# An attention and mixture-of-experts block: the routing stage written out per group of tokens, with a new order of work

## The reference, cut to what matters

```python
x = x + attn(layernorm(x))      # q, k, v = x @ wq.T, ...; 16 heads of 8
# qf, kf = elu(q) + 1, elu(k) + 1;  kv = sum over s of kf * v
# out = (qf @ kv) / (qf . sum(kf) + 1e-6);  then @ wo.T + bo
x = x + ffn(layernorm(x))       # 16 experts, top 2 of z @ router_w.T
# gates = sigmoid(top 2 logits)
# expert: (silu(z @ gate) * (z @ up)) @ down, scaled by the gate
# plus one shared expert of width 256 over all tokens
```

## Time and profile before

| what | value |
|---|---|
| median of 3 runs | 284.52 us (281.02 to 284.95) |
| profiled execution, span | 282.7 us (the page gives no other time for it) |
| PE busy, DVE busy, ACT busy, POOL busy | 214.7, 167.2, 124.3, 162.1 us |
| first scatter of the dispatch starts | 48.0 us |
| last scatter of the dispatch starts | 136.4 us |
| first block of the expert stage, PE | 145.3 us |
| last scatter of the expert stage starts | 255.7 us |

### The profile page before, as it was taken

One profiled execution on the slowest core, in us unless ns is written; L12 is line 12 of the kernel. 1 busy time (PEld: TensorE's weight loads), 2 busy tenths in 40 slices (PEclk: granted clock), 3 DMA queues, 4 the chain that ended last, 5 costly groups with the idle time before them and its releaser, 6 DMA issues.

```text
span 282.7 us, 5194 instructions
## 1 busy us (share of the span) xinstructions
PE 214.7 (76%) x1218; PEld 174.8 (62%) x1219; DVE 167.2 (59%) x670; ACT 124.3 (44%) x324; POOL 162.1 (57%) x164
## 2 busy tenths in 40 slices
PE   1677878887677557359949979899799799795561
PEld 0346676876566455247846768588587587594561
DVE  3337969678697787544326647647457466321582
ACT  2726465667648533050204635536455455420010
POOL 0454001757757666777301777777777777772780
PEclk9988959599999998856989999999999999999595
DMA  4225810111111111117733233333333333103993
GB/s 151 74 74 134 372 74 1 57 40 47 47 41 57 47 48 39 49 57 149 96 78 86 80 88 96 107 98 88 97 97 94 92 103 98 53 6 92 327 343 130
DMA packets 27876, 27.61 MB, mean 98 GB/s; under 512 B 4782, under 2 KB 25525, under 8 KB 27730
## 3 DMA queue, kind: packets, MB, share of 16 engines
q1 hardware_dynamic: 21954, 17.99, 22.4%
q0 software_dynamic: 4608, 8.47, 9.5%
q10 hardware_dynamic: 1296, 0.94, 1.6%
HBM read 15.70 MB, written 12.73 MB: 101 GB/s over the span
## 4 chain that ended last, share of the span: by engine, by line
PE 44%; DVE 17%; issue 12%; POOL 12%; DMA 8%; ACT 4%; SPq 1%; POOLq 0%; DVEq 0%; ACTq 0%
POOL routed L347 9%; PE pKVN L994 9%; PE pZ L988 6%; PE pQ L988 6%; DMA routed<-Z,ROWS 4%; PE pT L980 4%; PE pKV L853 3%; PE pT L983 3%; PE pZ L951 2%; POOL results L360 2%; PE pKVN L922 2%; DVE Z L558 2%; PE pKVN L843 2%; PE pN L843 2%; DVE c_stat L516 2%
## 5 line engine op out<-in xcount | busy, mean ns | idle before, releaser
L360 POOL DMA_INDIRECT results<-Y,XS x80 | 78.7, 984 | 40.5 <-ACT Y L466 21.3
L347 POOL DMA_INDIRECT routed<-Z,ROWS x64 | 62.0, 969 | 47.2 <-DVE ROWS L650 29.5
L730 DVE COPY xhT<-pT 128x256 f32<-128x256 f32 (+1 forms) x83 | 34.4, 414 | 20.6 <-PE pT L983 16.0
L994 PE MATMUL pKVN<-WF,xhT 128*128 x160 | 35.3, 302 | 1.5 <-ACT Y L466 1.5
L994 PEld LDWEIGHTS pKVN<-WF,xhT 128*128 128x128 f32 x160 | 26.3, 188 | 16.1 <-issue 14.5
L466 ACT ACTIVATE Y<-pKVN,XS 128x128 f32<-128x128 f32 x80 | 29.4, 367 | 5.6 <-PE pKVN L994 2.1
L980 PE MATMUL pT<-CN,XS 128*128 128x128 f32 x80 | 23.1, 289 | 11.4 <-issue 6.7
L853 PE MATMUL pKV<-WF,sh_h 128*128 128x128 f32 x128 | 20.9, 307 | 8.2 <-DVE X L746 8.2
L853 PEld LDWEIGHTS pKV<-WF,sh_h 128*128 128x128 f32 x128 | 19.1, 217 | 9.6 <-DVE sh_h L741 8.8
L988 PE MATMUL pZ<-WF,xhT 128*128 x80 | 24.8, 392 | 0.0
L988 PE MATMUL pQ<-WF,xhT 128*128 x80 | 24.4, 387 | 0.0
(11 more groups left out here) (124 smaller groups left out, 429.7 us busy)
## 6 DMA issues: line engine op xcount, KB each, us to landing
XS<-routed SPq DMA_DIRECT2D x80, 65.0 KB, 1.9
YL<-results SPq DMA_DIRECT2D x16, 256.0 KB, 5.8
WF<-w_ffn SPq DMA_DIRECT2D x1, 3456.0 KB, 12.0
X<-x SPq DMA_DIRECT2D x8, 256.0 KB, 2.7
out<-X SPq DMA_DIRECT2D x8, 256.0 KB, 2.9
results<-Y,XS POOLq DMA_INDIRECT x80, 2.3
routed<-Z,ROWS POOLq DMA_INDIRECT x64, 2.3
routed<-pad SPq DMA_DIRECT2D x11, 65.0 KB, 4.3
```

The source lines that it names most:

```text
L347: nc.gpsimd.indirect_dma_start(routed, bass.IndirectOffsetOnAxis(ap=ROWS[:, par, t, k:k + 1], axis=0), Z[:, par, t, k, :], None).then_inc( ...
L360: nc.gpsimd.indirect_dma_start(results, bass.IndirectOffsetOnAxis(ap=XS[:, j, D:D + 1].bitcast(U32), axis=0), Y[:, j, :], None, bounds_che ...
L730: nc.vector.tensor_copy(xhT[:, j % 2, a:b, :], pXH[:, a:b, :]).then_inc(s_xhT, 1)
L994: nc.tensor.matmul(pY, xhT[:, (j + 3) % 2, 1, :], WF[:, 2 * EXP_DIM:][:, bass.ds(w, D)], start=True, stop=True).then_inc(s_D, 1)
```

## The change

The two places of Z become eight, one for each quad, and so do the row numbers `ROWS`; the tile ZB that holds them is the same memory as `YL` of the end, which takes the place of a tile of its own. `norm2` no longer waits for scatters. The token numbers, which `route` copied into Z quad by quad (L610), are copied in one instruction before step 0. All eight loads of X are issued one behind the other, with a semaphore for each quad, and `WF` right behind them. PSUM's Z is copied straight into `ZT`, from which the logits are now computed; `zT` and its second copy are gone. The loop over pairs of steps, which made one turn, and POOL's loops are written out.

The order within a step changes on three engines. PE: state, keys, queries, numerators, transpose of Z, transpose of the tokens, logits, transpose of the attention, output projection, and the ranks of s-2 at the end of the step (before: of s-3, in the next step, behind the queries). DVE: residual, the row numbers and gates of s-3 at once, statistics, mask, the statistics of X with all that belongs to them (steps 0 to 2, one step earlier), the Newton instructions without anything between them, `norm2`, attention, `features_k`, `features_q`, `route`. ACT: the norm of the next tokens first, keys before queries.

```diff
+        ZB = sb("ZB", [P, NQ * QUAD * TOP_K * ROW])
+        Z = ZB[:, :].rearrange("p (q t k r) -> p q t k r", q=NQ, t=QUAD, k=TOP_K)
+        YL = ZB[:, 0:NQ * TOP_K * QTOK].rearrange("p (q k f) -> p q k f", q=NQ, k=TOP_K)
+        ysum = YL[:, :, 0, :]
...
-        zT = sb("zT", [P, QTOK])
...
-            sp.dma_start(quad(X, 0).rearrange("p (b f) -> p b f", b=SPQ), x_v[0]).then_inc(s_x, 16)
-            sp.dma_start(bo_row[0:1, :], bo).then_inc(s_bo, 16)
-            sp.wait_ge(s_x, 16)
-            with sp.Fori(1, NQ) as q:
-                sp.dma_start(quad(X, q).rearrange("p (b f) -> p b f", b=SPQ),
-                             x_v[bass.ds(q, 1)].rearrange("o p b f -> (o p) b f")).then_inc(s_x, 16)
-                wait_apart(sp, s_x, q * 16 + 16)
+            for q in range(NQ):
+                sp.dma_start(quad(X, q).rearrange("p (b f) -> p b f", b=SPQ), x_v[q]).then_inc(s_x[q], 16)
+                if q == 0:
+                    sp.dma_start(bo_row[0:1, :], bo).then_inc(s_bo, 16)
             sp.dma_start(WF[:, :], w_ffn).then_inc(s_wf, 16)
...
-            def dispatch(q, par):
+            for q in range(NQ):
...
-                            routed, bass.IndirectOffsetOnAxis(ap=ROWS[:, par, t, k:k + 1], axis=0),
-                            Z[:, par, t, k, :], None).then_inc(scat[par], 16)
-            with pool.Fori(0, NQ // 2) as it:
-                for par in range(2):
-                    dispatch(it * 2 + par, par)
+                            routed, bass.IndirectOffsetOnAxis(ap=ROWS[:, q, t, k:k + 1], axis=0),
+                            Z[:, q, t, k, :], None).then_inc(scat[q % 2], 16)
...
-                wait(act, a_kv, q - 1)
-                nc.scalar.copy(XNT[:, par, :], pT[:, :]).then_inc(a_xT, 1)
-            tokens_t(0, 0)
-            norm1(1, 1)
-            def step(s, par):
+                wait(act, a_q, q - 1)
+                nc.scalar.copy(XNT[:, q % 2, :], pT[:, :]).then_inc(a_xT, 1)
+            def step(s):
                 this, att_, last, coming = has(s, 0), has(s, 1), has(s, 2), has(s, -1)
+                if coming and s >= 0:
+                    norm1(s + 1)
                 if last:
                     rstd(c_mv, c_rs, c_aggr, c_ln, c_y, s - 2)
+                if stats(s):
+                    rstd(a_mv, a_rs, a_aggr, a_ln, a_y, s + 2, unit(s + 2))
                 if this:
+                    act.wait_ge(a_kv, s + 1)
+                    nc.scalar.activation(rk[:, :, :], pKVN[:, :, 0:D], ACT.Relu, scale=-1.0).then_inc(a_rk, 1)
+                    wait(act, b_kv, s - 1)
+                    nc.scalar.copy(V[:, s % 2, :, 0:D], pKVN[:, :, D:2 * D]).then_inc(a_v, 1)
+                    act.wait_ge(a_rk, s + 1)
+                    wait(act, a_kf, s)
+                    nc.scalar.activation(ek[:, :, :], rk[:, :, :], ACT.Exp, scale=-1.0).then_inc(a_ek, 1)
                     act.wait_ge(a_q, s + 1)
                     nc.scalar.activation(rq[:, :], pQ[:, :], ACT.Relu, scale=-1.0).then_inc(a_rq, 1)
+                if last:
+                    act.wait_ge(c_T, s - 1)
+                    nc.scalar.copy(quad(ZT, s - 2), pZ[:, :]).then_inc(c_zT, 1)
+                if this:
                     act.wait_ge(a_rq, s + 1)
                     wait(act, a_qf, s)
                     nc.scalar.activation(eq[:, :], rq[:, :], ACT.Exp, scale=-1.0).then_inc(a_eq, 1)
-                if stats(s):
-                    rstd(a_mv, a_rs, a_aggr, a_ln, a_y, s + 1, unit(s + 1))
-                if this:
-                    act.wait_ge(a_kv, s + 1)
-                    nc.scalar.activation(rk[:, :, :], pKVN[:, :, 0:D], ACT.Relu, scale=-1.0).then_inc(a_rk, 1)
-                if last:
-                    q = s - 2
-                    act.wait_ge(c_T, q + 1)
-                    wait(act, c_lg, q)
-                    nc.scalar.copy(zT[:, :], pZ[:, :]).then_inc(c_zT, 1)
-                if this:
-                    wait(act, b_kv, s - 1)
-                    nc.scalar.copy(V[:, par, :, 0:D], pKVN[:, :, D:2 * D]).then_inc(a_v, 1)
-                    act.wait_ge(a_rk, s + 1)
-                    wait(act, a_kf, s)
-                    nc.scalar.activation(ek[:, :, :], rk[:, :, :], ACT.Exp, scale=-1.0).then_inc(a_ek, 1)
                 if att_:
                     q = s - 1
                     act.wait_ge(b_T, q + 1)
                     wait(act, b_wo, q)
                     nc.scalar.copy(attT[:, :], pAT).then_inc(b_aT, 1)
-                if coming and not (isinstance(s, int) and s == 0):
-                    norm1(s + 1, 1 - par)
                 if last:
                     q = s - 2
                     act.wait_ge(c_top, q + 1)
                     wait(act, c_g1, q)
                     nc.scalar.activation(gate_e[:, :, :], top[:, :, 0:TOP_K], ACT.Exp, scale=-1.0).then_inc(c_ge, 1)
                     act.wait_ge(c_z, q + 1)
-                    nc.scalar.copy(Z[:, par, :, 1, 0:D], Z[:, par, :, 0, 0:D]).then_inc(c_zdup, 1)
+                    nc.scalar.copy(Z[:, q, :, 1, 0:D], Z[:, q, :, 0, 0:D]).then_inc(c_zdup, 1)
                 if coming:
-                    tokens_t(s + 1, 1 - par)
-                if last:
-                    q = s - 2
-                    act.wait_ge(c_zT, q + 1)
-                    nc.scalar.copy(quad(ZT, q), zT[:, :]).then_inc(c_zT2, 1)
-            steps(act, step)
+                    tokens_t(s + 1)
+            rstd(a_mv, a_rs, a_aggr, a_ln, a_y, 0, unit(0))
+            norm1(0)
+            rstd(a_mv, a_rs, a_aggr, a_ln, a_y, 1, unit(1))
+            for s in range(-1, NQ + 2):
+                step(s)
...
-            def norm2(q, par, dispatched):
+            def norm2(q):
                 dve.wait_ge(c_rstd, q + 1)
-                wait(dve, scat[par], dispatched)
-                for t in range(QUAD):
-                    i = nc.vector.tensor_scalar(Z[:, par, t, 0, 0:D], X1[:, bass.ds(q * QTOK + t * D, D)],
+                for t in range(QUAD):
+                    i = nc.vector.tensor_scalar(Z[:, q, t, 0, 0:D], X1[:, bass.ds(q * QTOK + t * D, D)],
...
-                nc.vector.tensor_copy(Z[:, par, :, :, D].bitcast(U32),
-                                      TOK[:, bass.ds(q * QUAD * TOP_K, QUAD * TOP_K)].rearrange("p (t k) -> p t k", k=TOP_K))
...
-                dve.wait_ge(c_ge, q + 1)
-                nc.vector.tensor_scalar(gate_1[:, :, :], gate_e[:, :, :], 1.0, None, ALU.add).then_inc(c_g1, 1)
                 dve.wait_ge(c_ch, q + 1)
                 with nc.allow_low_precision("counts up to 32 are exact in bfloat16"):
                     nc.vector.tensor_reduce(chosen_q[:, :], chosen[:, :, :].rearrange("p t e -> p e t"), AX.X, ALU.add).then_inc(c_chq, 1)
+            def gates1(q):
+                dve.wait_ge(c_ge, q + 1)
+                nc.vector.tensor_scalar(gate_1[:, :, :], gate_e[:, :, :], 1.0, None, ALU.add).then_inc(c_g1, 1)
+            def gates2(q):
                 dve.wait_ge(c_g1, q + 1)
-                nc.vector.reciprocal(Z[:, par, :, :, D + 1], gate_1[:, :, :]).then_inc(c_pay, 1)
+                nc.vector.reciprocal(Z[:, q, :, :, D + 1], gate_1[:, :, :]).then_inc(c_pay, 1)
...
+            def step(s):
+                this, att_, last, tail = has(s, 0), has(s, 1), has(s, 2), has(s, 3)
                 if last:
                     residual(s - 2)
+                if tail:
+                    rows1(s - 3)
+                    gates1(s - 3)
+                    rows2(s - 3)
+                    gates2(s - 3)
+                    rows3(s - 3)
+                if last:
                     wait_apart(dve, c_x1, s - 1)
                     bn_stats(X1, (s - 2) * QTOK, c_stat, c_stats)
                     bn_aggr(c_stat, c_mv, c_stats, c_aggr, s - 2)
                 if att_:
                     mask(s - 1)
                 if stats(s):
-                    wait_apart(dve, s_x, unit(s + 1).stop // QUAD * 16)
-                    bn_stats(X, 0, a_stat, a_stats, unit(s + 1))
+                    statistics(s + 2)
                 if last:
                     newton1(c_mv, c_rs, c_y, c_n1, s - 2)
-                if tail:
-                    rows1(s - 3)
-                if last:
                     newton2(c_rs, c_n1, c_n2, s - 2)
-                if tail:
-                    rows2(s - 3)
-                if last:
                     newton3(c_rs, c_n2, c_rstd, s - 2)
-                if tail:
-                    rows3(s - 3, 1 - par)
-                if last:
-                    q = s - 2
-                    if isinstance(q, int):
-                        dispatched = (q // 2) * 128
-                    else:
-                        dispatched = (q - 1) * 64 if par == 1 else q * 64
-                    norm2(q, par, dispatched)
+                    norm2(s - 2)
                 if stats(s):
-                    bn_aggr(a_stat, a_mv, a_stats, a_aggr, s + 1, unit(s + 1))
-                if this:
-                    features_q(s, par)
-                if stats(s):
```

(47 more changed lines are left out.)

214 lines of the change are left out of this document (93 added, 121 removed).

## The result

| | median of the runs | range | ratio to before on the same chip |
|---|---|---|---|
| before | 284.74 us | 281.02 to 285.0 (4 runs) | |
| changed | 275.8 us | 274.72 to 276.62 (4 runs) | 0.975 [0.970, 0.980] |

The change is worth 8.9 us. The forecast was 270.0 with a range of 266 to 277.5: the direction was right and 275.8 lies in that range, but the size was not right (14.5 us forecast), and the narrower range that the forecast gave for its own case, 266 to 273.5, does not hold it. The profiled run took 275.66 us with a span of 273.8, against 282.7 before, so the two spans differ by the same 8.9 us, and they can be taken apart. They are one execution each.

A forecast was written before the change was run, and what follows sets the result against it. The dispatch's scatters on POOL, in a ring of waits with DVE, were taken to bound the path before the expert stage. Start 6.5 plus gaps 8.0 gave 14.5 us: 284.5 to 270.0, range 266 to 277.5.

The forecast's parts named there:

- part B: POOL's gaps between quads of scatters, 8.2 us beyond the ordinary, vanish as steps fit POOL's 10.1 us; 8.0 us gained.
- part A: Start of the dispatch: first scatter at about 41.5 instead of 48.0, 6.5 us gained.
- R1: Rival: steps stay the bound, gaps stay as waits of PE and DVE, only the earlier start is gained; 278, chance 0.11.
- R3: Rival: early loads or a half-clock stretch before step 3 eat the start's gain, only the gaps' remains; 276.5, chance 0.08.
- (c): Row numbers before the first scatter: fewer instructions ahead, so they start 1.2 behind the residual instead of 4.7; 3.5 us earlier.
- R2: Rival: PE's clock falls to 1.2 GHz in every step, keys take 1.9 times as long; kernel 305, chance 0.04.
- (a): Step 0, keys before queries on PE: key features of quad 0 come earlier, between 1.8 and 2.5, taken as 2.3 us.
- R4: Rival: POOL's scatters get slower beside a denser DVE, 9 us in all; 279, chance 0.05.
- (b): Steps 1 and 2: work taken out between residuals of quads 0 and 1 brings 0.7 us; PE's clock may fall again.
- After the dispatch: Landing of the last scatter and the way to the expert stage: zero to 2.5 us more possible, none taken.

The follow-up runs named there:

- idle matmuls: Changed kernel plus identity-by-identity products on PE, results unused, where it would wait in the attention and routing stage: 269.73 us, ratio 0.950 to the kernel before.
- the control: The changed kernel itself, unedited, run again on another chip beside the kernel before: 277.5 us against 283.43, ratio 0.976.
- Eight Z alone: Kernel before with only eight places of Z and row numbers, no norm2 wait for scatters, loops written out; old order and X loads: 279.21 us, ratio 0.989.

## Why the prediction was wrong in its size

Two steps failed. The larger is in part B: the argument that PE keeps its full clock in the new steady steps because no gap there is as long as 1 us. B was put at 8.0 us and brought 3.4; with the clock held by idle matmuls it brought 88.44 - 79.96 = 8.5. The other is in part A: "The X loads cost and bring nothing in the sum". A was put at 6.5 and brought 3.7, and 2.4 in the control. That 275.8 lies in the range of 266 to 277.5 is luck in part: the upper end was set by R1 and R3, which came to 278 and 276.5, and neither is what happened.

Three readings of the prediction are not right, and change little: 64 x 1.26 is 80.6, not 80.9, and the row numbers start, not end, 4.7 us behind the residual (46.73 - 42.00), which is what (c) is worked out from. The 3.60 us of the keys were read as the low level, but the granted clock of 12 to 16 us is 1.00 in that trace, so only the duration speaks for it. Where the clock is 0.50 the output projection takes 2.08 us (at 39.69, changed kernel) against 1.16, 1.8 times as much, so R2's 1.9 was near.

**(a), keys before queries, 2.3 us: failed, by POOL's additions and by more.** The residual of quad 0 came 28.41 - 27.92 = 0.5 us earlier. The loads themselves were as harmless as said: WA landed after 3.8 us, 3.7 before. I followed them to the DMA engines and to the first use of WA, but not to the engine that they release. POOL's additions had been spread by the loads; released at once they lie beside the Newton instructions. With the additions held KF of quad 0 came at 16.17 instead of 17.72, and the residual 1.5 us earlier, 2.03 earlier than before. So much is shown.

Not all of the 2.03 belongs to the order, since the trace of the kernel before had the low clock within 19 to 23 us and this one had not. Of the traces of the changed kernel the control had it too, and its residual is at 29.20, 0.8 later than before. Eight Z alone, the old order without it, has the residual at 26.63: the changed kernel is 1.3 behind that, and 0.25 ahead with the additions held. At the same clock keys first is thus worth about 0.3 us at the residual by these single traces, not 2.3. The gain shrinks in two places. KF of the old order comes at 17.02 there, since its keys took 2.66 us and not 3.60, so 0.85 is left at KF. At `den` of quad 0 it is 22.27 against 22.52: DVE now waits 0.61 us for ACT ahead of the Newton instructions, where the old order had `features_q`.

The Trainium skill, "SBUF — State Buffer", section "Who interferes with whom", says that a DVE instruction with two SBUF inputs contends with a GpSimd instruction that reads SBUF, and one with a single SBUF input, outside the two-port modes, does not. The runs agree, in the direction opposite to my R4: 1.19 us against 0.17. Even before, one Newton instruction (at 24.42) took 0.52 us beside the addition that starts at 23.65:

```profile
24.42 0.52 DVE L535 SCALAR_TENSOR_TENSOR a_rs<-a_rs 128x8 f32<-128x8 f32 x1
```

**(b), steps 1 and 2, 0.7 us: the risk named came true.** Residuals 0 and 1 are 13.88 us apart, 13.59 before: -0.3. The wait of PE for `norm2` that was named is there, 2.21 us, and behind it PE runs at the low level:

```profile
34.56 0.96 PE L873 MATMUL pZ<-CN,ZB 128*128 128x128 f32 x4 [2.21 <-DVE ZB L523]
```

With idle matmuls in that gap the distance is 11.88 us, 1.7 less than before. But before ran these steps partly at the low level too; the old order at clock 1.00 (eight Z) has 39.05 - 26.63 = 12.42, so the order itself is worth 0.5 us, near the 0.7.

**(c), row numbers, 3.5 us: right.** From the residual of quad 1 to the first scatter it is now 44.28 - 41.80 = 2.48 us, 6.00 before: 3.52, and 2.48 in the control too. The three add up to 0.5 - 0.3 + 3.5 = 3.7.

**B, the gaps, 8.0 us: failed by the clock.** Its reasoning on DVE and PE at the full clock holds: 9.98 us in the changed kernel, 10.0 with the clock held, and then the last scatter starts at 122.29, as forecast. What failed is the argument against R2: "gaps of 1.08 us did not take the clock away, the one of 2.12 did, and the longest that I find in the new steady step ... is below 1". The length of the longest gap does not decide; the clock went at 82.26 behind a gap of 0.67 and after a step without a longer one. Nor did a gap of 2.12 us always take it away: in the trace of eight Z the same transposes behind the same gap run at 1.00, in 0.66 us where it was 1.12:

```profile
35.27 0.66 PE L942 MATMUL pKV<-CN,att 128*128 128x128 f32 x4 [2.12 <-DVE att L583]
```

I had also taken R2 as all or nothing, a low clock in every step, at 0.04. It is a low clock in some steps, it costs 5 us in the gaps where R2 had 35 (305 against 270), and this middle case was in none of the rivals. By the experiment with idle matmuls the clock took 7.0 us up to the last scatter (1.95 at the start, 5.04 behind it), of which 6.0 arrive in the span.

**After the dispatch, none taken, up to 2.5 as a bound:** 1.5 in this run, the same as the landing's 5.02 - 3.50, and within the scatter of that stretch from run to run.

**R1** names the old order rightly, not the new one, whose steps are 9.98 us at the full clock. **R3** did not hold: the start gained 3.7, and 2.4 in the control. **R4**: the longest of the 64 scatters is 1.110 us, the median 958 ns, as before; not so. What was to show the theory wrong, "gaps of 1 us or more in front of each quad", did in part: three of seven.

What stays open: why the clock falls in one steady step and not in the one before it. The runs show that more work on PE in the idle places keeps it, not which of PE's times decides. PE's busy time alone does not sort the steps either: from 72.34 to 82.26 us the changed kernel has PE busy for 8.54 us and then loses the clock, while the kernel before has 6.12 us in the same window and keeps 1.00 to 93 us.

## What to carry to other kernels

Where an order of work is changed, do not take PE's full clock for granted because the gaps are short, and count on losing it in some steps rather than in all or none; idle matmuls in the waits are a cheap test, and here also the cure, worth 6 to 8 us. Before a difference between two traces is put down to an edit, compare the granted clock of the same stretch in both: the kernel before and eight Z alone, which do the same work in the same order up to the first scatter, differ by 1.8 us at the first residual. When loads are issued earlier, follow them to the engine that they release and ask what then runs beside it: here an addition on GpSimd held an eight-element instruction on VectorE for about its whole 1.2 us. An experiment that frees time must be rid of everything that was sized for the old time.
